# A gated MLP and a linear layer with LoRA on one core: moving blocks loaded by ScalarE into five homes, LoRA A in two buffers, and two groups of operations placed earlier

## The reference, cut to what matters

```
y   = x + down                                 # x: 8 x 256 tokens, 1024 features, fp32
gate = x Wg^T + 0.5 (x Ag^T) Bg^T              # Ag, Bg chosen per batch row, rank 16
up   = x Wu^T + 0.5 (x Au^T) Bu^T              # 2752 hidden features
down = (silu(gate) * up) Wd^T + 0.5 (act Ad^T) Bd^T
out  = y + y Wo^T + bias + scale (y Al^T) Bl^T # Al, Bl, scale chosen per batch row
```

## Time and profile before

| | us |
|---|---|
| median of 3 runs (lowest, highest) | 1714.31 (1710.94, 1716.29) |
| profiled execution, whole | 1712.29 |
| its span in the profile | 1710.5 |
| TensorE busy | 1598.4 (93%) |
| VectorE busy | 1215.0 (71%) |
| GpSimd busy | 790.6 (46%) |
| ScalarE busy | 574.2 (34%) |

### The profile page before, as it was taken

The page is one execution under the profiler, slowest core; times in us unless marked ns, Lnnn a source line. Parts: engine busy times, 40 slices in busy tenths (PEclk is TensorE's granted clock), DMA queues, the critical chain, the costliest instruction groups (busy, mean ns, idle before and its releaser), DMA issues.

```text
span 1710.5 us, 21791 instructions
## 1 busy us (share of the span) xinstructions
PE 1598.4 (93%) x6820; PEld 1286.0 (75%) x6820; DVE 1215.0 (71%) x1538; ACT 574.2 (34%) x983; POOL 790.6 (46%) x571
## 2 busy tenths in 40 slices
PE   6989999999998999999999779997699998799998
PEld 4768887888887788878888557885477876578886
DVE  5988888888879888888886545865638646865343
ACT  3533333333445333334333223332233324431100
POOL 5244444444452544444444456773577763541110
PEclk9989999999999999999999889998899999899999
DMA  8344544534442345454334736447363334113322
GB/s 158 93 110 127 170 133 126 167 112 120 138 121 83 114 132 171 124 134 154 102 102 116 150 90 158 132 138 161 122 159 99 97 85 126 27 29 77 69 52 58
DMA packets 249813, 198.12 MB, mean 116 GB/s; under 512 B 114212, under 2 KB 203684, under 8 KB 249508
## 3 DMA queue, kind: packets, MB, share of 16 engines
q1 hardware_dynamic: 189696, 135.90, 32.1%
q10 hardware_dynamic: 59876, 60.83, 11.0%
q0 software_dynamic: 128, 0.00, 0.0%
HBM read 136.35 MB, written 60.29 MB: 115 GB/s over the span
## 4 chain that ended last, share of the span: by engine, by line
PE 51%; DVE 8%; issue 3%; DMA 2%; SPq 2%; ACT 1%; POOL 1%; ACTq 0%; DVEq 0%
PE ps L2328 51%; DVE Ad_turned L1252 2%; SPq L1594 1%; DVE acc L1182 1%; DMA raw<-in_L_cond_W_down_dram 1%; DMA Ad_raw<-in_L_cond_A_down_dram 1%; DMA raw<-xt_scratch 1%; DVE s L682 0%; POOL W L2197 0%; DVE s L689 0%; DVE Tr L1169 0%; SPq L1549 0%; DVE TU L656 0%; DVE xt L721 0%; DVE tw_down L1280 0%
## 5 line engine op out<-in xcount | busy, mean ns | idle before, releaser
L2328 PE MATMUL ps<-X_T,W 128*128 128x512 f32 x1944 | 464.7, 394 | 19.5 <-DVE vbuf L880 8.4
L2328 PE MATMUL ps<-Tr,Sr 128*128 128x512 f32 x1680 | 416.2, 403 | 49.7 <-DVE acc L1182 15.8
L2328 PEld LDWEIGHTS ps<-X_T,W 128*128 128x128 f32 x1944 | 366.8, 190 | 105.2 <-DVE vbuf L880 15.4
L2328 PE MATMUL ps<-X_B,W 128*128 128x512 f32 x1728 | 421.7, 394 | 18.7 <-ACT X_B L1760 12.9
L2328 PEld LDWEIGHTS ps<-Tr,Sr 128*128 128x128 f32 x1680 | 325.9, 195 | 132.6 <-issue 21.5
L2328 PEld LDWEIGHTS ps<-X_B,W 128*128 128x128 f32 x1728 | 328.1, 190 | 90.7 <-issue 14.4
L2197 POOL TENSOR_TENSOR W<-s,W 128x512 fp32r<-128x512 f32 x156 | 211.5, 1359 | 224.7 <-ACT W L1731 224.6
L2238 POOL TENSOR_TENSOR Tr<-st,Tr 128x512 fp32r<-128x512 f32 x140 | 197.9, 1415 | 170.7 <-ACT Tr L1966 170.6
L2197 POOL TENSOR_TENSOR W<-TG,W 128x512 fp32r<-128x512 f32 x88 | 122.6, 1394 | 232.3 <-ACT W L1731 232.2
L1966 ACT ACTIVATE Tr<-st 128x512 fp32r<-128x512 f32 x160 | 99.7, 630 | 330.9 <-PE ps L2328 252.8
L1731 ACT ACTIVATE W<-s 128x512 fp32r<-128x512 f32 x156 | 98.4, 632 | 226.0 <-PE ps L2328 222.6
(11 more groups left out here) (155 smaller groups left out, 1790.7 us busy)
## 6 DMA issues: line engine op xcount, KB each, us to landing
raw<-in_L_cond_W_gate_dram SPq DMA_DIRECT2D x164, 128.0 KB, 3.0
raw<-in_L_cond_W_up_dram SPq DMA_DIRECT2D x164, 128.0 KB, 3.2
st<-sums_scratch SPq DMA_DIRECT2D x80, 256.0 KB, 2.8
st<-act_scratch SPq DMA_DIRECT2D x80, 256.0 KB, 3.4
raw<-in_x_dram SPq DMA_DIRECT2D x104, 128.0 KB, 3.1
raw<-in_L_cond_W_down_dram SPq DMA_DIRECT2D x88, 128.0 KB, 3.9
act_scratch<-c21buf ACTq DMA_DIRECT2D x42, 256.0 KB, 2.4
act_scratch<-vbuf ACTq DMA_DIRECT2D x42, 256.0 KB, 3.0
```

Of the source, the lines that this page charges most:

```text
L2328: return nc.tensor.matmul(dst, stationary, moving, start=start, stop=stop, skip_group_check=True)
```

## The change

1. *Moving blocks.* `load_moving` goes from SyncE's stream into ScalarE's. ScalarE loads four blocks ahead in `last_unit`, and then block n+4 right behind its own copy of block n. There are five homes `st`; the load waits for the low part of block n-1. The fifth home lies where the buffer of the activation sums (`t1buf`) was.
2. *LoRA A.* `Ad_raw` has two buffers with a semaphore each; SyncE loads blocks 0 and 1 before the last unit, and a later one when the turn two before it is over. Blocks 1 and 2 are turned at steps 1 and 4 in place of 3 and 5.
3. *First weights.* VectorE turns LoRA A 0 at the end of the last full unit, and both halves of weights 1 around the first operation of the half tile. ScalarE makes LoRA A 0 and `down_step(-3)` before the silu of the half tile; the parts of weights 1 are made one step later (at -2) than those of weights 0.
4. *Last block.* The first LoRA sum (`td_copy(0)`, `td_first(0)`) is made within the last steps, before the last banks are read. The second (`td_first(1)`) and the turns of Bd 2 and 3 come behind the low parts of the first. `bd_low(0)` and `bd_low(1)` go from VectorE to GpSimd, with a semaphore of their own. TensorE runs four tiles before the first `down_adapter` in place of three, and two adapters behind each of tiles 3 and 4.

The diff, cut to its core:

```diff
@@ -20,7 +20,7 @@
...
-STAGING = 4
+STAGING = 5
...
-        st = [at(f"st{j}", 65536 + 2048 * j, [P, TT]) for j in range(STAGING)]
+        st = [at(f"st{j}", 65536 + 2048 * j if j < 4 else 209632, [P, TT]) for j in range(STAGING)]
...
-        Ad_raw = at("Ad_raw", 147456, [P, FB])
+        Ad_raw = [at(f"Ad_raw{j}", o, [P, FB]) for j, o in enumerate((147456, 211680))]
...
-        AD_STEP = {1: 3, 2: 5, 3: 7, 4: 9, 5: 68, 6: 70, 7: 72, 8: 74, 9: 76, 10: 100}
+        AD_STEP = {1: 1, 2: 4, 3: 7, 4: 9, 5: 68, 6: 70, 7: 72, 8: 74, 9: 76, 10: 100}
...
+        bd_lo, bd_lo2 = sem("bd_lo"), sem("bd_lo2")
+        ad_loaded = [sem(f"ad_loaded{j}") for j in range(2)]
+        ad_turned, ad_hi, ad_lo = (sem(n) for n in ("ad_turned", "ad_hi", "ad_lo"))
...
@@ -1065,6 +1066,8 @@
                 if h == 1 and u == FULL - 1:
                     turn_down(0, 0)
                 add_c12(U)
+                if h == 1 and u == FULL - 1:
+                    turn_ad(0)
...
@@ -1081,12 +1084,10 @@
                     half_tile_first(U)
                 else:
                     turn_down(0, 1)
+                    turn_down(1, 0)
                     half_tile_first(U)
-                    turn_ad(0)
+                    turn_down(1, 1)
                 half_tile_second(U)
-                if h == 1:
-                    turn_down(1, 0)
-                    turn_down(1, 1)
...
-                        eng.wait_ge(bd_lo, earlier[1] + 1)
+                        eng.wait_ge(*((bd_lo, earlier[1] + 1) if earlier[1] < 2 else (bd_lo2, earlier[1] - 1)))
...
@@ -1233,16 +1234,18 @@
                         turn_ad(bb)
                 if q in (STEPS - 3, STEPS - 2):
                     last_low(q - STEPS + 3)
+                if q == STEPS - 1:
+                    td_first(0)
...
-                                ALU.subtract).then_inc(bd_lo, 1)
+                                ALU.subtract).then_inc(bd_lo2, 1)
 
             def turn_ad(bb):
-                eng.wait_ge(ad_loaded, (bb + 1) * NB * 16)
+                eng.wait_ge(ad_loaded[bb % 2], (bb // 2 + 1) * NB * 16)
...
@@ -1311,6 +1314,9 @@
                         td_mask(0)
                         td_low(0, 0)
                         td_low(0, 1)
+                        td_first(1)
+                        for p in range(2, 4):
+                            turn_item(("Bd", p))
...
@@ -1453,12 +1459,6 @@
             second_act(ALL - 1)
             for q in range(-3, STEPS + 3):
                 down_step(q)
-            for pr in range(2):
-                td_first(pr)
-            for p in range(2):
-                bd_low(p)
-            for p in range(2, 4):
-                turn_item(("Bd", p))
             last_block()
...
-                else:
-                    sp.wait_ge(ad_turned, bb)
+                elif bb > 1:
+                    sp.wait_ge(ad_turned, bb - 1)
...
-            def load_moving(n):
...
-                for n, moving in enumerate(MOVING):
-                    if moving[0] == q + 6:
-                        load_moving(n)
                 for item in raw_at_step(q + 4):
...
-                for bb in range(1, BLOCKS):
+                for bb in range(2, BLOCKS):
                     if AD_STEP[bb] == q + 4:
                         load_ad(bb)
...
                     if item == ("D", 0, 0):
                         load_ad(0)
+                        load_ad(1)
                     elif item == ("D", 1, 1):
...
@@ -1945,17 +1926,39 @@
                     silu_second(U - 1)
                     w_high(U + 1, "A11")
                     x_high(1, "B11", 0)
+                else:
+                    for n in range(STAGING - 1):
+                        load_moving(n)
+                    ad_high(0)
                 store_act(U - 1)
+                if h == 1:
+                    down_step(-3)
                 silu_first(U)
                 if h == 0:
                     w_high(U + 1, "A12")
                     x_high(1, "B21", 0)
                     w_high(U + 1, "A21")
                     w_high(U + 1, "A22")
-                else:
-                    ad_high(0)
...
+            def load_moving(n):
+
+                _, name, j, h = MOVING[n]
+                if n >= STAGING:
+                    wait_mv_low(eng, n - STAGING)
+                elif n < 4:
+                    wait_stage(eng, ALL - 2, "P5")
+                else:
+                    eng.wait_ge(t_stored[1], 16 * HALVES * (BLOCKS - 1))
+                if name[0] == "B":
+                    t, c = 2 * j + int(name[1]) - 1, int(name[2]) - 1
+                    eng.wait_ge(act_stored[c], 16 * (h * UNITS + t + 1))
+                    src = act_d[t, :, h * T + c * TT:h * T + (c + 1) * TT]
+                else:
+                    i = int(name[1]) - 1
+                    eng.wait_ge(t_stored[i], 16 * (h * (BLOCKS - 1) + j + 1))
+                    src = tt_d[i, j, :, h * TT:(h + 1) * TT]
+                eng.dma_start(st[n % STAGING][:, :], src).then_inc(mv_loaded[n % STAGING], 16)
...
@@ -2015,7 +2018,9 @@
                 for n in range(len(MOVING)):
                     if mv_step(n) == q:
                         moving_high(n)
-                for n in {-3: (0, 1), -1: (2,), 0: (3,), 1: (4,)}.get(q, ()):
+                        if n + STAGING - 1 < len(MOVING):
+                            load_moving(n + STAGING - 1)
+                for n in {-3: (0,), -2: (1,), -1: (2,), 0: (3,), 1: (4,)}.get(q, ()):
                     still_high(STILL[n])
                 if still_for(q - 1) is not None:
                     still_high(still_for(q - 1))
...
+                if q == STEPS - 3:
+                    td_copy(0)
...
-                eng.wait_ge(tb_added.sem, tb_added.after(T_STAGES[-1]))
+                eng.wait_ge(tb_added.sem, tb_added.after(T_STAGES[pr - 2]))
...
             store_act(ALL - 1)
             for q in range(-2, STEPS):
                 down_step(q)
-            td_copy(0)
-            td_copy(1)
             bd_high(0)
             bd_high(1)
+            td_copy(1)
             td_high(0)
             bd_high(2)
...
+            def bd_low(p):
+                eng.wait_ge(it_hi.sem, it_hi.after((("Bd", p), 0)))
...
+                                ALU.subtract).then_inc(bd_lo, 1)
...
-                for n in {-3: (0, 1), -1: (2,), 0: (3,), 1: (4,)}.get(q, ()):
+                for n in {-3: (0,), -2: (1,), -1: (2,), 0: (3,), 1: (4,)}.get(q, ()):
...
             ad_low(0)
             for q in range(-3, STEPS):
                 down_step(q)
+            bd_low(0)
+            bd_low(1)
             for k in range(KT):
...
-                eng.wait_ge(bd_lo, 2 * pr + 2)
+                eng.wait_ge((bd_lo, bd_lo2)[pr], 2)
...
                     down_tile(dst, s)
                     down_half_tile(dst, s)
                     waiting.append(s)
-                    if (k, pr) in ((0, 0), (1, 0)):
+                    if pr == 0 and k < 3:
                         continue
                     down_adapter(waiting.pop(0))
-                    if (k, pr) == (3, 0):
+                    if pr == 0 and k < 5:
                         down_adapter(waiting.pop(0))
                 down_adapter(waiting.pop(0))
```

More of the change, by code:

```diff
@@ L1253, in turn_ad @@
                             Ad_turned[q * Q:(q + 1) * Q, :, w, :],
-                            Ad_raw[w * Q:(w + 1) * Q, :].rearrange("p (z i) -> p z i", i=Q)[:, groups, :])
+                            Ad_raw[bb % 2][w * Q:(w + 1) * Q, :].rearrange("p (z i) -> p z i", i=Q)[:, groups, :])
                 last.then_inc(ad_turned, 1)
@@ L2251, in full_low @@
                                 ALU.subtract).then_inc(full_lo, 1)
+            def bd_low(p):
+                eng.wait_ge(it_hi.sem, it_hi.after((("Bd", p), 0)))
+                G.tensor_tensor(Bd[p][2 * Q:3 * Q, :, :].rearrange("p k (q i) -> p q k i", q=NQ),
+                                turned[t_at["Bd", p] % 2][0:Q, :].rearrange("p (q k i) -> p q k i", q=NQ, k=KT),
+                                Bd[p][0:Q, :, :].rearrange("p k (q i) -> p q k i", q=NQ).bitcast(F32),
+                                ALU.subtract).then_inc(bd_lo, 1)
             def down_step(q):
```

20 lines of the change are left out of this document (2 added, 18 removed).

## The result

The changed kernel takes 1671.94 us (median of 4 runs, 1667.31 to 1672.33) against 1714.23 (1710.94 to 1716.29) in the same round: ratio 0.9749, 95% interval 0.9726 to 0.9772, 42.3 us less. In a second round it measured 0.977 [0.9746, 0.9794]. The forecast was 1657 us, and a gain of 56.5 us in one execution; the profiled executions differ by 40.2 (span 1710.5 to 1670.3).

The account below looks back on a forecast made before the run. TensorE sets the end, losing 85.7 us to idling and lower clock in three thin stretches. Gains 17+25+7+7.5 = 56.5 took the profiled 1712.3 to 1655.8; the median, 2.0 higher, gave 1657.8, stated as 1657; range 1638 to 1684.

Parts of the forecast that it names:

- three thin stretches: TensorE at 940 to 1010, 1164 to 1239 and 1420 to 1480 us: 31.1, 32.6 and 22.0 us lost, idle and lower clock.
- Step 0 begins at 947.8, step 1 at 954.7: Start of the down projection: step 0 follows the last unit, removing a 5.78 us gap; step 1 waits for its moving block.
- Block 3 is turned at 959.3 and block 4 at 965.1: Start, weight chain through three raw buffers: turn 1.30, four issues 2.0 to 2.9, landing 3.9 us; step 4 starts at 967.1.
- lower bound of 10: Start: gain of 10 us in place of 17 if weight landings lengthen by 1.5 us in each of the last rounds.
- Rival A: Chance 0.12: waits are for transfers, not the queue's order; moving blocks and raw loads come no earlier; gain 22, 1692 us.
- SyncE no longer waits for moving blocks, so raw loads start when their buffer is free: Middle, 1164 to 1239 us: residual and weight loads start three items ahead; lost 8 in place of 32.6, gain 25 us.
- Steps 61 to 69 lose about 1 us: Middle, P7, where each step takes two moving blocks: only about 1 us of TensorE time stays lost.
- 5 us stay: Middle, steps 70 to 76: VectorE needs 20.5 us until step 75's bank, TensorE 15.6, so 5 us of waiting remain.
- I put back 2 us for GpSimd: Late stretch: GpSimd's 3.6 us against 3.21 in two steps costs 2 us; gain 7 from the second-last block's earlier load.
- LoRA sums: Last block: sums and turns reordered, Bd low parts on GpSimd; gaps of 1.5 and about 4.6 us stay, gain 7.5.
- ScalarE's issues: ScalarE's 156 new loads at 0.33 us each, 1.26 at worst, hide in 1.5 us free per step: no cost.
- C's: Rival, chance 0.02: slower; ScalarE's queue sets the pace, waiting for low parts; 140 steps each 0.5 us longer, 1728 us.

## Why the prediction was right, and where it fell short

- **Direction and most of the size: right.** The three thin stretches of the earlier trace rows held the gain; before them and after them nothing moved (0.1 us each).
- **"Step 0 begins at 947.8, step 1 at 954.7": right** (947.46, 955.10).
- **"Block 3 is turned at 959.3 and block 4 at 965.1": failed, the start's whole shortfall.** They were turned by 964.4 and 969.7, 5.1 and 4.6 us late. I took one landing of 3.9 in series with one turn and four issues; with the issues no longer held up, landings take 5.2 (median) and the issues themselves longer. The lower bound of 10 named it; I took 17. Rival A was thus right for what is left of the start, and wrong for what went. My argument against it, DMA busy 0.56 of the time, was a mean over 70 us: from 950 to 970 us, where the late weights were under way, the share was 0.95 in the kernel before.
- **"SyncE no longer waits for moving blocks, so raw loads start when their buffer is free": right as an effect, wrong as to the part.** I gave the middle's gain to the new issuer. The runs give it to two waits in one queue. With one LoRA A buffer left, the new issuer and the fifth home together give 10.2 us; with two buffers the new issuer gives 23.7.
- **"Steps 61 to 69 lose about 1 us": failed.** One weight landed 3.10 us late in P7, where each step takes two moving blocks, and cost TensorE 3.77 us and over 1 us of low clock (three matmuls in 1.63 us). Its four loads took 4.8 to 8.2 us to land, at a DMA share of 1.04 between 1150 and 1160. "5 us stay" at step 75: 5.32, right.
- **"I put back 2 us for GpSimd" in the late stretch: mis-sized.** Three gaps of 4.5 us in all and 1.5 us of low clock (4.43 for twelve matmuls at 1395). SyncE, free now, issues the second-last block, eight Bd pieces and four of Wo within some 9 us, and a moving block takes 5.5 us to land, for which ScalarE stands 3.21; then it waits for GpSimd, which has 2.4 us of full_low in two of these steps. With the halves two steps later, full_low on VectorE and Bd behind it the stretch is 182.0.
- **LoRA sums: the gaps were right (1.5 and 4.6; measured 0.50 and 5.11), the sum was not.** 6.1 us of gaps against 10.4 make 4.3, not 7.5: I let the low clock behind the gap disappear with it. It follows the new one as well: ten matmuls at 1427 take 4.4 us, where at 1433 they take 2.3. Measured 4.7.
- **ScalarE's issues: 0.** Right to within some 5 us, as the run with SyncE as issuer shows.
- **The signs named beforehand: most came, and three that spoke against me.** VectorE has no wait for LoRA A, the gap near 1420 is gone, and the gaps around the first adapter products are 0.50 and 5.11. But the weights at the start land later than 4 us (5.2), ScalarE stands 3.21 us once for a moving block (A's sign), and it waits for GpSimd's low parts (C's). Of the 31.1 and 32.6 us lost in the two thin stretches 18.8 and 12.1 stay, where 8 to 14 were forecast. The total lies in the range all the same, 15 us above the forecast. Two sums in the prediction are slightly off and change nothing: 5x2.75+2 is 15.75, and 1657.8 was given as 1657.
